# A two-layer attention and expert kernel: the first layer's feed-forward computed for the chosen experts only, and every second damage strain on TensorE

## Time and profile before

| what | us |
|---|---|
| median of 3 runs | 1205.12 (1204.17 to 1207.86) |
| profiled execution, first to last instruction | 1203.6 |
| setup | 0 to 41 |
| strain loop, group 0 | 41 to 328 |
| band block, group 0 | 328 to 406 |
| strain loop, group 1 | 406 to 693 |
| band block, group 1 | 693 to 773 |
| second layer | 773 to 1204 |

### The profile page before, as it was taken

How to read it: one execution, slowest core, us unless ns; L and a number is a source line. 1 busy time by engine, 2 the same in 40 slices (tenths; PEclk the granted TensorE clock), 3 DMA queues, 4 the chain that set the end, 5 groups by cost and what they waited for, 6 DMA issues and landing times. The chain is left out here.

```text
span 1203.6 us, 23755 instructions
## 1 busy us (share of the span) xinstructions
PE 1056.1 (88%) x9995; PEld 567.0 (47%) x9995; DVE 962.4 (80%) x1193; ACT 821.7 (68%) x888; POOL 168.1 (14%) x265
## 2 busy tenths in 40 slices
PE   6499888998879499889899868999999999999897
PEld 4233333333368333333333368853654565655533
DVE  7899999999763799999999863557778577676757
ACT  3689999999763489999989862243156666665464
POOL 5100000000140100000000050232760000000072
PEclk9699999999979789999999979999779999999899
DMA  8400000000075200000000057000132344523121
GB/s 269 128 2 2 1 1 2 1 1 2 1 204 145 54 1 2 1 1 2 1 1 2 1 172 178 24 1 1 36 105 62 105 132 125 155 80 90 47 60 45
DMA packets 71754, 67.45 MB, mean 56 GB/s; under 512 B 6148, under 2 KB 63200, under 8 KB 71648
## 3 DMA queue, kind: packets, MB, share of 16 engines
q1 hardware_dynamic: 66264, 55.31, 16.1%
q0 software_dynamic: 3840, 10.43, 3.3%
q10 hardware_dynamic: 1544, 0.20, 0.1%
HBM read 41.80 MB, written 20.97 MB: 52 GB/s over the span
## 5 line engine op out<-in xcount | busy, mean ns | idle before, releaser
L580 DVE SCALAR_TENSOR_TENSOR ring<-AD,PT 128x1808 f32<-128x1808 f32 (+15 forms) x128 | 286.1, 2235 | 3.8 <-POOLq L562 1.9
L725 PE MATMUL LG<-ring,lred 128*32 128x456 f32 (+15 forms) x2048 | 233.4, 575 | 2.0 <-ACT ring L677 2.0
L1932 DVE TENSOR_REDUCE MX<-SS 128x2 f32<-128x1024 f32 x119 | 144.6, 1219 | 55.3 <-PE SS L1649 55.2
L1862 ACT ACTIVATE EX<-SS 128x1024 f32<-128x1024 f32 x128 | 130.4, 1031 | 80.4 <-PE SS L1649 79.8
L667 ACT ACTIVATE ring<-ring 128x3616 f32<-128x3616 f32 (+15 forms) x50 | 169.9, 3398 | 3.7 <-DVE ring L580 3.7
L747 PE MATMUL SD<-DS,eyes 96*32 96x456 bf16 (+15 forms) x2496 | 156.2, 369 | 10.1 <-ACT ring L672 8.1
L675 ACT ACTIVATE ring<-ring 128x1824 f32<-128x1824 f32 (+15 forms) x78 | 141.0, 1808 | 0.0
L747 PEld LDWEIGHTS SD<-DS,eyes 96*32 96x32 bf16 x2496 | 58.0, 96 | 154.6 <-ACT ring L672 56.7
L580 DVE SCALAR_TENSOR_TENSOR ring<-AD,bdmg 128x1808 f32<-128x1808 f32 (+15 forms) x50 | 111.4, 2228 | 0.0
L725 PEld LDWEIGHTS LG<-ring,lred 128*32 128x32 f32 x2048 | 59.4, 110 | 100.2 <-issue 76.6
L760 PE MATMUL PY<-w2T,xg 128*128 128x128 f32 x512 | 75.6, 292 | 31.5 <-DVE xg L605 31.5
(11 more groups left out here) (346 smaller groups left out, 1558.0 us busy)
## 6 DMA issues: line engine op xcount, KB each, us to landing
w1s<-in_L_ffn_W SPq DMA_DIRECT2D x39, 256.0 KB, 3.0
w2s<-in_L_ffn_W SPq DMA_DIRECT2D x39, 256.0 KB, 2.9
band<-zs SPq DMA_DIRECT2D x8, 1024.0 KB, 9.9
wide<-band POOLq DMA_DIRECT2D x16, 380.0 KB, 8.3
wide<-band SPq DMA_DIRECT2D x16, 380.0 KB, 10.0
band<-Z SPq DMA_DIRECT2D x4, 1024.0 KB, 7.7
xs<-Z SPq DMA_DIRECT2D x4, 640.0 KB, 8.0
xl<-xs SPq DMA_DIRECT2D x10, 256.0 KB, 2.9
```

What stands on the lines that cost most here:

```text
L580: return v.scalar_tensor_tensor(out=ring[:, slot, s, :, t0:T], in0=AD[:, s, :, j + t0:j + T], scalar=extra, in1=AD[:, s, :, PAD + t0:PAD + T],
L725: mm = pe.matmul(LG[32 * b:32 * b + 32, par, s, t0:T], lred[:, s, n % 4, :], ring[:, slot, s, b, t0:T], start=(n % 4 == 0), stop=(n % 4 == 3))
L1862: act.activation(EX[:, Q % 2, hh:hh + 2, t, :], SS[:, slot, :, :], ACT.Exp, scale=SCALE1).then_inc(freed[slot], 1)
L1932: v.tensor_reduce(MX[:, t, p // 2, hh:hh + 2], pairs_of(b, name), AX.X, ALU.max).then_inc(freed[slot], 1)
```

## The change

`PE_ITEMS` becomes every second item (4 of 8; 3 in the first iteration). The first layer's feed-forward is no longer dense. Each row is copied to a slot of `xs0` for each of its 4 experts (64 indirect transfers by POOL in the strain loop of group 0, 128 rows each), the slots of an expert fill whole tiles of 128 rows (79 tiles, padded to 80), and the tiles are worked in 20 groups of 4: 8 groups in iterations 4 to 7 of the first loop, 12 in iterations 0 to 5 of the second, two an iteration (A and B). For a group: SP loads 512 rows (`tokens`, one buffer `xl`) and 4 + 4 weight tiles by registers (`weights1`, two buffers; `weights2`, one buffer), PE turns the rows (`turn`), they are moved to `xsT` (`move_in`), then `hidden`, `glu_in`, `sig`, `glu_out`, `expert_out`, `move_out`, and SP stores the group (`store`). At the end 64 indirect gathers bring the result rows back, and 64 DVE instructions (`add_rows`) add them to `ACC` by gate: gates 0 and 1 in the second loop, gates 2 and 3 in the second band block. The zeros for `band` and `xs` move from the setup to SP's queue in the first loop; in the setup SP zeroes `xs0` (5.2 MB) and writes the two turned weight tensors to memory. Slots and tables are worked out in the first iteration of the first loop (`count`, `starts`, `tables` on PE, `expert_tiles`, `token_slots`, `tile_tables` on DVE).

The diff, cut to its core:

```diff
-PE_ITEMS = (1, 2, 4, 6, 7)
-AFTER_PE = (2, 7)
-FIRST_PE_ITEMS = (2, 4, 6, 7)
+PE_ITEMS = (1, 3, 5, 7)
+FIRST_PE_ITEMS = (3, 5, 7)
 NPE = len(PE_ITEMS)
 LOOP_PE = 7 * NPE + len(FIRST_PE_ITEMS)
+TILES0 = B * T * K0 // P + E0 - 1
+GROUPS0 = -(-TILES0 // 4)
+NTILE0 = 4 * GROUPS0
+ROWS0 = NTILE0 * P
+ZQ = 12
+MOE_ITS = ((4, 5, 6, 7), (0, 1, 2, 3, 4, 5))
...
+            for i in range(NTILE0 * C // 2048):
+                sp.dma_start(flat[:, 2048 * i:2048 * i + 2048], zeros).then_inc(d_xs0, 16)
+            sp.wait_ge(d_small, 64)
+            sp.wait_ge(mlp_sb, 4)
+            sp.dma_start(w1d.rearrange("e p i -> p e i"), w1T[:]).then_inc(d_small, 16)
+            sp.wait_ge(mlp_sb, 8)
+            sp.dma_start(w2d.rearrange("e p c -> p e c"), w2T[:]).then_inc(d_small, 16)
...
+    def gather(pool, k, half, dst):
+        for t in range(8 * half, 8 * half + 8):
+            pool.indirect_dma_start(dst[:, t, :], None, ys0[:, :], bass.IndirectOffsetOnAxis(ap=sloti[:, t, k:k + 1], axis=0),
+                                    bounds_check=ROWS0 - 1, oob_is_err=True).then_inc(d_yg[half] if k < 3 else d_yh, 16)
+    def add_rows(v, k, half, src):
+        if k < 3:
+            v.wait_ge(d_yg[half], 16 * 8 * (k + 1))
+        else:
+            v.wait_ge(d_yh, 16 * TT)
+        if k:
+            v.wait_ge(added, 2 * k + half - 1)
+        for t in range(8 * half, 8 * half + 8):
+            a = ACC[:, t, :]
+            ins = v.scalar_tensor_tensor(out=a, in0=src[:, t, :], scalar=gates0[:, k, t:t + 1], in1=a, op0=ALU.mult, op1=ALU.add)
+        ins.then_inc(added, 1)
...
+                def tokens(n):
+                    sp.wait_ge(tok_turned, n)
+                    sp.dma_start(xl[:], xs0[4 * P * n:4 * P * n + 4 * P, :].rearrange("(n p) c -> p n c", p=P)).then_inc(d_xl, 16)
+                def weights1(n):
+                    if n >= 2:
+                        sp.wait_ge(h_ready, n - 1)
+                    for a in range(4):
+                        e = sp.value_load(owneri[0:1, 4 * n + a:4 * n + a + 1], min_val=0, max_val=E0 - 1)
+                        sp.dma_start(w1s[:, n % 2, a, :], w1d[bass.ds(e, 1), :, :].rearrange("o p i -> p (o i)")).then_inc(d_w1[n % 2], 16)
+                def weights2(n):
+                    if n:
+                        sp.wait_ge(y_ready, n)
+                    for a in range(4):
+                        e = sp.value_load(owneri[0:1, 4 * n + a:4 * n + a + 1], min_val=0, max_val=E0 - 1)
+                        sp.dma_start(w2s[:, a, :], w2d[bass.ds(e, 1), :, :].rearrange("o p c -> p (o c)")).then_inc(d_w2, 16)
+                def store(n):
+                    sp.wait_ge(y_used, n + 1)
+                    sp.dma_start(ys0[4 * P * n:4 * P * n + 4 * P, :].rearrange("(n p) c -> p n c", p=P), yo[:]).then_inc(d_ys, 16)
                 sp.wait_ge(ds_zero, g + 1)
...
+                for n, ready, count in ((0, parts_act, 1), (1, parts_act, 2), (2, parts_dve, 2)):
+                    sp.wait_ge(ready, 2 * g + count)
                     for q in range(4):
                         sp.dma_start(DS[32 * n:32 * n + 32, q, :, PAD:PAD + T], parts[n][32 * q:32 * q + 32]).then_inc(d_parts, 16)
+                if g == 0:
+                    zeros = Z[:, ZQ:JQ, :]
+                    for par in range(NT):
+                        sp.dma_start(band[par].rearrange("p (g r) -> p g r", g=NG)[:, :, 4 * WIN:],
+                                     zeros.rearrange("p q t -> p (q t)").rearrange("p (g r) -> p g r", g=NG)).then_inc(d_zero, 16)
...
+                    sp.wait_ge(d_small, 96)
+                    sp.wait_ge(small_pool, 6)
+                weights1(groups[0])
+                weights2(groups[0])
+                if g == 0:
+                    sp.wait_ge(d_scatter, 16 * TT * K0)
+                tokens(groups[0])
+                for n in groups:
+                    if n + 1 in groups:
+                        weights1(n + 1)
+                        tokens(n + 1)
+                        weights2(n + 1)
+                    store(n)
+                sp.wait_ge(d_ys, 16 * (groups[-1] + 1))
...
+                    pool.wait_ge(small_pool, 5)
+                    pool.wait_ge(d_xs0, 16 * (NTILE0 * C // 2048))
+                    for t in range(TT):
+                        for k in range(K0):
+                            pool.indirect_dma_start(xs0[:, :], bass.IndirectOffsetOnAxis(ap=sloti[:, t, k:k + 1], axis=0), TF[:, t, :], None,
+                                                    bounds_check=ROWS0 - 1, oob_is_err=True).then_inc(d_scatter, 16)
+                else:
+                    pool.wait_ge(d_ys, 16 * GROUPS0)
+                    for k in range(2):
+                        for half in range(2):
+                            if k:
+                                pool.wait_ge(added, 2 * k + half - 1)
+                            gather(pool, k, half, yg0)
...
+                def move_in(n):
+                    if n is not None:
+                        v.wait_ge(tok_turned, n + 1)
+                        v.tensor_copy(xsT[:], PH[:]).then_inc(tok_moved, 1)
+                def glu_in(n):
+                    if n is not None:
+                        v.wait_ge(h_ready, n + 1)
+                        if n:
+                            v.wait_ge(y_ready, n)
+                        for a in range(4):
+                            ins = v.tensor_scalar(xg[:, P * a:P * a + P], PH[:, P * a:P * a + P], b1s[:, 4 * n + a:4 * n + a + 1], LIMIT,
+                                                  ALU.add, ALU.min)
+                        ins.then_inc(xg_ready, 1)
+                def glu_out(n):
+                    if n is not None:
+                        v.wait_ge(sig_ready, n + 1)
+                        v.scalar_tensor_tensor(out=xg[:], in0=t2[:], scalar=1.0, in1=xg[:], op0=ALU.add, op1=ALU.mult).then_inc(s_ready, 1)
+                def move_out(n):
+                    if n is not None:
+                        v.wait_ge(y_ready, n + 1)
+                        if n:
+                            v.wait_ge(d_ys, 16 * n)
+                        v.tensor_copy(yo[:], PY[:]).then_inc(y_used, 1)
                 def body(it):
...
+                    A, B_ = moe_groups(g, it)
+                    before = moe_groups(g, it - 1)[1] if it else None
+                    item(4, it)
+                    item(5, it)
+                    move_out(before)
                     if it:
                         logits(1, 2 * it - 1)
...
+                    item(6, it)
+                    glu_in(A)
+                    if (g, it) == (0, 0):
+                        token_slots()
+                    if (g, it) == (1, 7):
+                        add_rows(v, 0, 0, yg0)
+                    item(7, it)
+                    move_in(B_)
+                    item(8, it)
+                    glu_out(A)
                     logits(0, 2 * it)
...
+                    if (g, it) == (0, 0):
+                        tile_tables()
+                    item(9, it)
+                    glu_in(B_)
+                    if (g, it) == (1, 7):
+                        add_rows(v, 0, 1, yg0)
+                    item(10, it)
+                    move_out(A)
+                    item(11, it)
+                    glu_out(B_)
+                    if (g, it) == (1, 7):
+                        add_rows(v, 1, 0, yg0)
...
+                def sig(n):
+                    if n is not None:
+                        act.wait_ge(xg_ready, n + 1)
+                        act.activation(t2[:], xg[:], ACT.Tanh, scale=ALPHA / 2).then_inc(sig_ready, 1)
+                def move_in(n):
+                    if n is not None:
+                        act.wait_ge(tok_turned, n + 1)
+                        act.copy(xsT[:], PH[:]).then_inc(tok_moved, 1)
                 def body(it):
...
+                    A, B_ = moe_groups(g, it)
                     gelu(2, it)
+                    move_in(A)
                     gelu(3, it)
                     gelu(4, it)
...
+                    sig(A)
                     gelu(5, it)
                     gelu(6, it)
                     tanh(0, 2 * it)
...
                     gelu(7, it)
...
+                    gelu(8, it)
+                    sig(B_)
+                    gelu(9, it)
                     tanh(1, 2 * it + 1)
...
+                def turn(n):
+                    if n is not None:
+                        pe.wait_ge(d_xl, 16 * (n + 1))
+                        pe.wait_ge(xg_ready, n)
+                        for a in range(4):
+                            mm = pe.transpose(PH[:, P * a:P * a + P], xl[:, a, :], ident[:])
+                        mm.then_inc(tok_turned, 1)
+                def hidden(n):
+                    if n is not None:
+                        pe.wait_ge(tok_moved, n + 1)
+                        pe.wait_ge(d_w1[n % 2], 64 * (n // 2 + 1))
+                        for a in range(4):
```

(57 more changed lines are left out.)

418 lines of the change are left out of this document (219 added, 199 removed).

## The result

The changed kernel takes 1390.13 us (median of 4 runs, 1372.41 to 1394.96) against 1204.64 of the kernel before on the same chip (1202.84 to 1207.86). The ratio is 1.145, 95% interval 1.138 to 1.151; it is taken from the two quicker runs (1372.41 and 1386.67), since the two others lie over 1.5% above the quickest and count as slow. The forecast was 1365 with a range of 1275 to 1400, and the result lies inside it. The profiled execution has a span of 1384.9 us against 1203.6.

A forecast was written before the change was run, and what follows sets the result against it. DVE, busy 33.00 of 33.00 us, bounded the strain loops; after the change a chain of waits would. 1203.6 + 57 (loop 0) + 89 (loop 1) + 14 (band block 1) = 1364, with 1.5 for the median 1365 us; range 1275 to 1400.

The forecast's parts named there:

- The circle: Loop iterations with experts: the closed chain of waits through SP, PE and DVE, 43.8 us, 47.5 with PE's low clock.
- The halves: Two parts of an expert iteration: B's turn to next A's, 25.9 us; A's turn to B's, 17.9 us.
- loop 1: Second strain loop, expert iterations then remaining items and the gathers behind them: 376 us, +89.
- The first turn: Loop 0: PE's first `turn` needs all 64 scatters and ends at 205 us, bounds 168 and 235.
- I take one wait for the end of a strain for each scatter: Loop 0, POOL beside DVE strains: some 13 scatters an iteration, 41 by 167 us, 20 left at 1.27.
- Rival (a): Loop 0: scatters are not held up, first turn at 168, 37 us earlier; total 1328 us; chance 0.18.
- Rival (d): Loop 0: two waits for each scatter; total 1395 us; chance 0.06.
- Band block 1: Second band block: 16 gathers, 21 us, stand before POOL's first read, so PE's turn comes at 735.5: +14.
- `add_rows` uses DVE time that is idle: Second band block: DVE's additions of gathered rows fall in idle time, with no us put down for them.
- The faster case: Loops: tokens land about 5 us after their turn's place in PE's queue, engines bound; total 1183 us; chance 0.08.
- the ring's slack: Strain loops: item j waits for item j-4's reduction, up to 12 us of DVE work away, hiding engine hand-overs.
- the likeliest case: Whole kernel: the main forecast of 1365 us, spanning 1335 to 1390 by iterations of 45 to 50; chance 0.58.

The follow-up runs named there:

- early tokens: Changed kernel with a second token buffer; SP issues tokens and `weights1` of group n + 2 ahead of `weights2` of n + 1: 1302.2 us, ratio 1.081.
- tokens first: Changed kernel with one swap on SP, tokens issued ahead of `weights1`, buffer still single: 1314.1 us, ratio 1.091.
- The pause: Changed kernel with one added DVE wait after the tile tables, until POOL has written `owneri`: 1371.1 us, ratio 1.139.
- run 20: Not a run number: the text reads "in that run", then "20 scatters"; that run is the changed kernel with one added DVE wait, 1371.1 us.
- the quarter run: Changed kernel with 16 scatters issued and awaited in place of 64, other dispatched rows left zero: 1332.1 us, ratio 1.108.
- the late turn: Early tokens kernel with `turn(B)` on PE moved from ahead of reduce(4) to behind it: 1304.8 us, ratio 1.078.

## Why the prediction was right, and where its terms were off

**The circle** (47.5 us an iteration; measured 45.6 to 48.1) is shown three ways: by the intervals, by early tokens, which removes it, and by tokens first, which takes out one term and shortens it by that term. That followed from the earlier trace rows and the order of the calls, without any engine being busier. The halves agree too: from tokens to tokens SP takes 19.8 us (589.25 to 609.08) and 27.8 (561.42 to 589.25), for 17.9 and 25.9 with 1.8 of clock each. Inside them two terms were off and nearly cancel: four register loads in a row take 3.6 us and not 4.5 (the 1.13 of the earlier trace rows is the step from a store to the load behind it), and that step, here 1.14 us, was put at 0.6. From store to tokens this gives 4.8 for 5.1. One part was over-counted: the first circle of a loop is 39 to 42 us, since nothing of SP but `weights1` lies between the tokens of A and of B there (503.50 and 508.35). That is most of the 13 us by which loop 1 (+76, forecast +89) came out shorter.

**The first turn** (205, measured 226.6). The step that failed is "I take one wait for the end of a strain for each scatter", and `owneri`, which stands ahead of them, was in no sum at all. `owneri` and the first two scatters were shut out across five to seven strains each. The later ones beside strains are as forecast, at a pitch of mostly 2.13, and the last 36 lie 1.27 apart while DVE stands still. The pause gives 19 of those 22 us back and puts the turn at 206.7; in that run 20 scatters are left at 1.27, just as forecast. Rival (a), no hold-up, was wrong on the pitch; the quarter run shows what its 168 would be worth. Rival (d), two waits for each scatter, has a total of 1395 nearer to the 1390 than the forecast's 1365, but not its mechanism.

The Trainium skill (SBUF — State Buffer, section "Who interferes with whom") has the lock between two-SBUF-input DVE instructions and GpSimd's reads. The same page of the Trainium skill (section "SBUF: two separate sides") says that whichever of the two starts first has the shared ports for its whole instruction, and the other blocks. The pitch agrees, 2.13 us beside strains for 1.27 alone. The three long waits do not: there POOL stayed blocked when the first strain had finished, and through four to six more.

**Band block 1** (+14, measured +28). The read behind 16 gathers cost 18.4 us at the first turn, for 15.6 expected, and the rows after it were at the low clock (1.95 us for 1.13). "`add_rows` uses DVE time that is idle" was wrong: 926.54 and 941.39, 2.19 us each, stood ahead of DVE's copies for PE, and each of these two turns is some 3 us longer. DVE in band block 1:

```profile
925.83 0.68 DVE L1158 TENSOR_TENSOR ACC<-ACC,WB 128x512 f32<-128x512 f32 x1
926.54 2.19 DVE L578 SCALAR_TENSOR_TENSOR ACC<-yg,gates,ACC 128x128 f32<-128x128 f32 x8
928.64 0.68 DVE L1146 COPY wtT<-WB 128x512 f32<-128x512 f32 x1
```

**The faster case** (1183) asked for tokens within the ring's slack. With the circle gone (early tokens) the loops are 310 and 325, not near 260. An iteration with experts takes 34.8 us at the least where its sum has DVE bound at 32.3; DVE is busy for 31.0 of them, and what sets the rest is open, since neither the late turn nor a strain less on DVE gave it back. And the scatters hold the first turn in any case (44.1 us of waiting with early tokens). The sum did count the 16 more strains of the alternating items on DVE, which cost 30 us measured alone. Even repaired, no version with the dispatch reached 1205.

**The total** is better than its parts. Loop 0 was 22 us over its forecast, band block 1 14 over, loop 1 13 under and the setup 3 under: 21 of span in all, and part of that closeness is luck. The result also lies at the upper edge of the 1335 to 1390 that I gave the likeliest case.

## What to carry to other kernels

When a change puts loads, tokens and stores of one group in one in-order queue with single buffers, walk the circle once from a turn to the next and add it up: if it is longer than the busiest engine's iteration, it is the iteration, and less work on the engines is worth nothing. Look first for a term that needs no place in the circle; here two swapped lines were worth some 68 us. Where small GpSimd work has to start beside a DVE stream without a pause, try a pause at its start; 0.63 us was enough here in all five versions that had it. And before a difference between two versions is put down to the edit, look in both profiles for what came by chance, as the first turn did here.

## What the runs showed of the hardware that I had not expected

- GpSimd can be shut out by back-to-back DVE instructions with two SBUF inputs for 8.3 to 15.6 us, over up to seven of them (half-length ones too). With a pause of 0.63 us on DVE ahead of the first scatter it was not seen in any of five profiles; without one it was seen in six of seven. What starts it is open.
- Beside strains each scatter takes 1.8 us at a pitch of 2.13, that of the strains; with strains in two halves it takes 1.95 at 2.25.
- DVE's strains show next to no price for this: one of 1856 columns takes 2.15 us beside scatters and 2.13 while POOL is shut out, as the 2.15 of the earlier trace rows.
- The kernel before differs by 4% between chips (1204 and 1257 us). On the slower chip the second layer, the same in all versions, ran at PEclk 0.88 in 488 us, on the others at 0.94 to 0.96 in 430 to 435; the loops took no longer there.
